# Decoder layer on one Trainium2 core: order of the prologue, copies into the stacks, and a narrower first score product

## The chip, the cores and the metric

The kernel runs on one NeuronCore of a Trainium2 chip. The core has TensorE (PE, matrix products into PSUM), VectorE (DVE), ScalarE (ACT), GpSimd (POOL) and SyncE (SP); in this kernel SP only issues transfers, nearly all of them, in one queue that is worked in program order. The metric is the device time of one launch in microseconds (us). Lower is better.

## The reference

One decoder layer over 64 sequences of 256 tokens with 256 features, with a context of 120 tokens per sequence, all in float32:

```python
x = x + self_attention(layernorm(x))          # 16 heads of 16, bias -slope_h * |i - j|, causal
x = x + cross_attention(layernorm(x), ctx)    # 16 heads of 16 over the 120 context tokens, no mask
x = x + tanh(layernorm(x) @ W @ A1 @ A2 + bias)
```

Self-attention of one head is `softmax(q @ k.T / 4 + bias) @ v`, where a key later than the query is excluded (minus infinity). So for 256 queries and 256 keys the quarter "first 128 queries, last 128 keys" is excluded as a whole, and two quarters are cut along their diagonal.

## The kernel before, in words

**The precision scheme.** Most products run in a rounded 32-bit format (`fp32r` in the trace's operand column of what is written, `f32` in that of a matmul). An operand is split into a high half, rounded by ScalarE (`hi`, line 774), and a low half, the rest, made by VectorE (`lo`, line 920). A semaphore `K_hi`, `Q_hi`, `XQ_hi` counts the high halves and `K_lo`, `Q_lo`, `XQ_lo` the low ones. VectorE works on a block only after ScalarE has.

**The stacks.** For scores the 16 dimensions of a head are laid out 128 partitions high in `q_stack` and `k_stack` (two of each, for even and odd sequences) and in `xq_stack` and `xk_stack`. In each group of 8 rows, rows 0, 4 and 1 (`TRIPLE`) hold high and low halves of the 16 dimensions; rows 2, 3, 5 and 6 (`STEPS`) hold constants whose products make the causal mask; 7 and 15 hold the distance bias; the last row holds the shift, minus the row's maximum. So one matmul gives the shifted, biased and masked score. `restack` (line 422) fills the three rows of `TRIPLE` by three transfers of 256 KB each, from `q_nat` or `k_nat`: before it issues any, SP waits for the low half, and for the last reader of the stack.

**The mask constants.** `steps_q` and `steps_k` (lines 1062 to 1073, GpSimd) hold 64 patterns over 256 tokens, four tokens to a pattern (`NSTEP = 4`). `set_rows(p)` (line 367) copies them, the ones and the bias rows into the stacks of parity p with 11 transfers, of which 8 are of 256 KB.

**Score products.** For each head `scores` (line 617) does two matmuls into one PSUM bank: keys 128 to 255 against all 256 queries (line 622), and keys 0 to 127 against all 256 queries (line 623). The exponential (line 805) reads columns 128 to 511 of the bank, so not the first 128 columns, the excluded quarter. `maxima` (line 576) forms the same scores in bf16 for the row maxima, on stacks without the shift row; VectorE reduces them (line 962), `MAX_T` transposes them (line 613), ScalarE copies them out (line 844) and SP's `MAX_STACK` (line 435) puts them into the shift row with two transfers.

**Order of the work.** Nothing is planned at run time: `ORDER` (line 65) is for each engine a list of steps with an offset in sequences, and every engine walks its list for t from -2 to 65, so that three sequences are under way at a time. All engines take their instructions strictly in program order. For t from 6 to 61 the walk is a hardware loop of two sequences.

**The prologue.** It differs from the loop in what is put around it. SP first loads x, all weights, the bias rows (`alibi`, in four pieces) and the biases in the order of line 354. PE, ACT and DVE turn and split the weights of `FIRST` (q, k and two of the feed-forward weights); then each engine walks its list; and in front of the first step that `comes_first` (line 296) does not let through, it runs `after_first`: on PE, ACT and DVE `other_weights`, the rest of the weights; on SP `other_rows` (line 388), that is a wait for three tiles zeroed by GpSimd, `set_rows(1)` and one more transfer; on POOL `other_zeroes` (line 1081), the zeroing of `k_stack[1]`, `q_stack[1]` and `xk_stack`. Before its walk ACT waits for the bias rows, all nine biases and the scaled biases (lines 763 to 765); DVE waits for the nine biases and scales two of them (lines 910 to 913); POOL waits for the nine biases (line 1078).

SP's list for a step t is `LOAD_X` (t+1), `MAX_STACK` (t), `XK_STACK` (t-1), `LOAD_CTX` (t), `XQ_STACK` (t-1), `K_STACK` (t+1), `Q_STACK` (t+1), `XMAX_STACK` (t-1), `STORE` (t-2), `XK_SAVE` (t). POOL's is `FFN` (t-2), `LN2` (t), `LN1` (t+2), `LN3` (t-1). Of a sequence's 16 `SCORE` steps in PE's list, six stand right behind a product whose operands are all in the rounded format: heads 1, 3, 7, 8, 9 and 11.

Of the kernel before, what the change touches and what calls it, by code (L numbers as in the profile page):

```python
# [31 lines left out]
ALU = mybir.AluOpType  # L32
# [7 lines left out]
H = 16  # L40
# [9 lines left out]
NSTEP = 4  # L50
UP = [2.0 ** (57 - 38 * p) for p in range(NSTEP)]
DOWN = [0.0] + [-2.0 ** (38 * p - 82) for p in range(1, NSTEP)]
BEYOND = -2.0 ** 70
# [115 lines left out]
def build(nc, x, ctx, wts, bias, alibi, out):  # L169
    turns = bank_turns()  # L170
    with ExitStack() as stack:
# [37 lines left out]
        steps_q = sb("steps_q", [T // NSTEP, T])  # L209
        steps_k = sb("steps_k", [T // NSTEP, T])  # L210
# [85 lines left out]
        def comes_first(kind, b):  # L296

            return kind in ("LOAD_X", "LOAD_CTX", "LN1", "LN1_T", "K", "Q") or \
                kind in ("K_STACK", "Q_STACK") and b == 0

        def walk(eng, name, do, after_first):

            def step(i, t):
                for kind, b, part in step_order(name, t):
                    do[kind](i, b, part)
            waiting = True
            for t in range(FIRST_STEP, LOOP_FROM):
                for kind, b, part in step_order(name, t):
                    if waiting and not comes_first(kind, b):
# [42 lines left out]
        def _(sp):  # L352
            sp.dma_start(x_in[0][:, :, :], x[0].rearrange("(a p) d -> p a d", p=P)).then_inc(sem("x_loaded0"), 16)
            for n in ["q", "k", "alibi", "f1", "f0", "f2", "v", "o", "xq", "xk", "xv", "xo"]:
# [12 lines left out]
            def set_rows(p):  # L367
# [7 lines left out]
                for stacks, made in ((q_stack, steps_q), (k_stack, steps_k)):  # L375
                    for n, row in enumerate(STEPS):
                        sp.dma_start(stacks[p][row:P:ROWSTEP, :, :].bitcast(F32),
                                     made[n::NSTEP, :].unsqueeze(1).to_broadcast([P // ROWSTEP, H, T]))\
                            .then_inc(set_, 16)
# [5 lines left out]
            sp.wait_ge(sem("steps_cut"), 2)  # L385
# [58 lines left out]
            def store(i, b, _):  # L444
# [7 lines left out]
                "Q_STACK": restack("q", "Q_lo", q_nat, q_stack, (0, 0, 1)),  # L452
                "K_STACK": restack("k", "K_lo", k_nat, k_stack, (0, 1, 0)),
                "XQ_STACK": restack("xq", "XQ_lo", q_nat, [xq_stack] * 2, (0, 0, 1)),
# [9 lines left out]
        def _(pe):  # L464
# [26 lines left out]
            def other_weights():  # L491

                first = [(k, b) for t in range(FIRST_STEP, LOOP_FROM) for k, b, _ in step_order("PE", t)]
                first = first[:[comes_first(k, b) for k, b in first].index(False)]
# [122 lines left out]
            def scores(i, b, h):  # L617
# [4 lines left out]
                pe.matmul(bk[:, 0:T], ks[:, h, P:T], qs[:, h, :], start=True, stop=True)  # L622
# [109 lines left out]
        def _(act):  # L732
# [41 lines left out]
            def hi(kind, free):  # L774
# [3 lines left out]
                def f(i, b, _):  # L778
# [4 lines left out]
                    free(i, b)  # L783
                    bk = blocks(bank_of(kind, i, b))
# [93 lines left out]
        def _(dve):  # L878
# [33 lines left out]
            dve.tensor_scalar(bcol["xq"][:, :], bcol["xq"][:, :], SCALE["xq"], None, ALU.mult)\  # L912
                .then_inc(sem("b_scaled"), 1)
# [6 lines left out]
            def lo(kind):  # L920
# [3 lines left out]
                def f(i, b, _):  # L924
                    if kind in ("CTX_T", "XK"):
# [130 lines left out]
        def _(pool):  # L1056
# [5 lines left out]
            for p in range(NSTEP):  # L1062
                pool.memset(steps_q[:, p::NSTEP], UP[p]).then_inc(sem("steps_laid"), 1)
                pool.memset(steps_k[:, p::NSTEP], DOWN[p]).then_inc(sem("steps_laid"), 1)
            pool.wait_ge(sem("steps_laid"), 2 * NSTEP)
            for tile in (steps_q, steps_k):
                pool.affine_select(out=tile[:, :], in_=tile[:, :], compare_op=ALU.is_ge, fill=0.0, base=0,
                                   pattern=[[1, T]], channel_multiplier=-NSTEP).then_inc(sem("steps_from"), 1)
            pool.wait_ge(sem("steps_from"), 2)
            for tile, beyond in ((steps_q, 0.0), (steps_k, BEYOND)):  # L1070
                pool.affine_select(out=tile[:, :], in_=tile[:, :], compare_op=ALU.is_ge, fill=beyond,
                                   base=NSTEP - 1, pattern=[[-1, T]], channel_multiplier=NSTEP)\
                    .then_inc(sem("steps_cut"), 1)
# [4 lines left out]
            pool.wait_ge(sem("b_loaded"), 16 * 9)  # L1078
# [8 lines left out]
            def normalise(kind, src, dst, free, bias_name, biased):  # L1087
# [3 lines left out]
                def f(i, b, _):  # L1091
# [84 lines left out]
```

## Time and profile before

| | |
|---|---|
| median of three runs | 2411.53 us (2410.28 to 2416.39) |
| the profiled execution | 2413.22 us |
| its span, first to last instruction | 2411.4 us |
| PE busy | 2235.1 us, 93% |
| PE weight loads busy | 1850.9 us, 77% |
| DVE, ACT, POOL busy | 1710.2, 1416.4, 719.4 us |
| DMA | 244.83 MB moved, mean 102 GB/s |
| mean granted TensorE clock | 0.979 of 2.4 GHz |

The span is the time from the first to the last instruction; the profiled execution's own time is 1.8 us more. A group of instructions in the profile shows its line, engine, operation and operands. Matmuls overlap: the recorded duration of one is longer than the distance from its start to the next one's start. The chain of waits gives a matmul the time by which it moved the chain on, and so does not count the overlap.

### The profile page before, as it was taken

Reading aid. Unit: us, or ns where it says so; the run is one execution under the profiler, and the core shown is the slowest. Engines: PE = TensorE matmul, PEld = TensorE weight load, DVE = VectorE, ACT = ScalarE, POOL = GpSimd, SP = SyncE. Lnnn points to the kernel's source line nnn. Section 1 sums busy time; section 2 is a strip of 40 time slices with the busy share of each in tenths; the row PEclk is TensorE's granted clock in tenths of the full one; section 3 lists DMA queues with packets and bytes.
Section 4 is the critical chain, followed back from the end, with each engine's and each line's share of the span. In section 5 each row is a group of like instructions: output and inputs, shape, how many; then the busy total and the mean of one; then the engine's idle time right before and its main releaser. Section 6 shows DMA issues by size and latency. Waiting matters only on the chain.

```text
span 2411.4 us, 67050 instructions
## 1 busy us (share of the span) xinstructions
PE 2235.1 (93%) x22072; PEld 1850.9 (77%) x22072; DVE 1710.2 (71%) x3710; ACT 1416.4 (59%) x3066; POOL 719.4 (30%) x1371
## 2 busy tenths in 40 slices
PE   3489999999999999999999999999999999999985
PEld 2367887887788788788878878887887888788774
DVE  3167777777777777777777778777777877777762
ACT  2246666666666666666666666666666666666651
POOL 1223233233333323323332332333233233323321
PEclk9699999999999999999999999999999999999996
DMA  7333443443343344334334433433443343344320
GB/s 126 76 81 104 115 109 95 111 109 97 99 118 105 97 111 109 96 100 118 104 98 111 109 93 102 115 103 101 111 109 89 106 114 101 105 111 109 89 81 22
DMA packets 167370, 244.83 MB, mean 102 GB/s; under 512 B 22176, under 2 KB 90512, under 8 KB 164248
## 3 DMA queue, kind: packets, MB, share of 16 engines
q1 hardware_dynamic: 165660, 244.22, 38.2%
q8 instruction: 28, 0.46, 0.1%
q10 hardware_dynamic: 1664, 0.01, 0.1%
q14 instruction: 18, 0.15, 0.0%
HBM read 53.13 MB, written 33.56 MB: 36 GB/s over the span
## 4 chain that ended last, share of the span: by engine, by line
PE 74%; DVE 8%; POOL 4%; DMA 4%; issue 4%; SPq 2%; ACT 2%; DVEq 0%; POOLq 0%; ACTq 0%
PE ps_misc L534 13%; PE ps_misc L548 13%; PE ps_score L622 7%; PE ps_max L605 5%; PE ps_score L632 5%; PE ps_score L623 4%; PE ps_attend L647 4%; PE ps_misc L677 4%; DVE neg_max_s L962 4%; PE ps_max L593 4%; PE ps_misc L518 3%; PE ps_misc L692 3%; PE ps_attend L666 2%; DMA q_stack<-neg_max_t_s 2%; PE ps_misc L559 2%
## 5 line engine op out<-in xcount | busy, mean ns | idle before, releaser
L805 ACT ACTIVATE probs<-ps_score 128x384 f32<-128x384 f32 x1024 | 476.0, 494 | 177.4 <-PE ps_score L623 174.2
L962 DVE TENSOR_REDUCE neg_max_s<-ps_max 128x2 f32<-128x512 f32 (+1 forms) x768 | 479.5, 680 | 5.5 <-PE ps_max L587 4.1
L812 ACT ACTIVATE xprobs<-ps_score 120x512 f32<-120x512 f32 x512 | 292.4, 597 | 251.9 <-PE ps_score L632 213.8
L622 PE MATMUL ps_score<-q_stack,k_stack 128*128 128x256 f32 x1024 | 343.0, 345 | 46.4 <-DMA q_stack<-neg_max_t_s 42.3
L1095 POOL TENSOR_SCALAR ve_LN<-mv_LN 128x2 f32<-128x2 f32 x192 | 37.0, 193 | 1152.1 <-DVE mv_LN L984 1146.5
L970 DVE TENSOR_REDUCE neg_max_x<-ps_max 128x4 f32<-128x480 f32 x512 | 317.0, 651 | 25.7 <-PE ps_max L605 14.1
L623 PE MATMUL ps_score<-q_stack,k_stack 128*128 128x256 f32 x1024 | 279.6, 281 | 0.0
L622 PEld LDWEIGHTS ps_score<-q_stack,k_stack 128*128 128x128 f32 x1024 | 194.1, 190 | 92.3 <-DMA q_stack<-neg_max_t_s 58.5
L632 PE MATMUL ps_score<-xq_stack,xk_stack 128*120 128x256 f32 x1024 | 201.7, 309 | 3.7 <-DMA xq_stack<-neg_max_t_x 2.8
L1121 POOL TENSOR_TENSOR res<-res,chain_n 128x512 f32<-128x512 f32 x64 | 81.7, 1276 | 412.6 <-ACT chain_n L850 412.6
L593 PE MATMUL ps_max<-k_stack,q_stack 127*128 127x256 bf16 x1024 | 195.7, 282 | 4.1 <-DVE neg_max_s L962 0.6
L623 PEld LDWEIGHTS ps_score<-q_stack,k_stack 128*128 128x128 f32 x1024 | 196.3, 192 | 0.0
L605 PE MATMUL ps_max<-xk_stack,xq_stack 127*128 127x120 bf16 x2048 | 183.7, 219 | 5.8 <-DMA xq_stack<-q_nat 5.3
L632 PEld LDWEIGHTS ps_score<-xq_stack,xk_stack 128*120 128x120 f32 x1024 | 138.9, 183 | 59.7 <-ACT xprobs L812 27.7
L936 DVE TENSOR_TENSOR chain_t<-ps_misc,chain_t 128x512 fp32r<-128x512 f32 x128 | 88.2, 689 | 119.0 <-ACT chain_t L790 119.0
L822 ACT ACTIVATE heads_t<-ps_attend 128x512 f32<-128x512 f32 x256 | 152.7, 597 | 24.3 <-PE ps_attend L666 15.5
L677 PE MATMUL ps_misc<-ident,heads_t 128*128 128x128 f32 x1024 | 159.8, 279 | 6.3 <-ACT heads_t L822 1.8
L647 PE MATMUL ps_attend<-probs,v_aug 128*32 128x256 f32 x2048 | 164.4, 393 | 0.0
L945 DVE SCALAR_TENSOR_TENSOR q_nat<-ps_misc,bias_xq,q_nat 128x256 fp32r<-128x256 f32 x128 | 56.1, 479 | 145.0 <-ACT q_nat L798 145.0
L666 PE MATMUL ps_attend<-xprobs,xv_aug 120*32 120x256 f32 x2048 | 152.1, 392 | 2.4 <-ACT heads_t L822 1.4
L1109 POOL TENSOR_SCALAR chain_n<-res,rstd_LN,nmr_LN 128x256 f32<-128x256 f32 x256 | 141.2, 559 | 27.1 <-POOL nmr_LN L1104 27.1
L605 PEld LDWEIGHTS ps_max<-xk_stack,xq_stack 127*128 127x128 bf16 x2048 | 120.4, 98 | 27.5 <-DVE neg_max_x L970 6.3
(147 smaller groups left out, 5394.0 us busy)
## 6 DMA issues: line engine op xcount, KB each, us to landing
k_stack<-k_nat SPq DMA_DIRECT2D x192, 256.0 KB, 3.6
q_stack<-q_nat SPq DMA_DIRECT2D x192, 256.0 KB, 3.7
xq_stack<-q_nat SPq DMA_DIRECT2D x192, 256.0 KB, 3.7
xk_stack<-scr_xk SPq DMA_DIRECT2D x192, 128.0 KB, 2.7
x_in<-in_x SPq DMA_DIRECT2D x64, 256.0 KB, 2.7
scr_xk<-k_nat SPq DMA_DIRECT2D x32, 512.0 KB, 3.0
out_y<-res SPq DMA_DIRECT2D x64, 256.0 KB, 2.2
ctx_in<-in_ctx SPq DMA_DIRECT2D x32, 240.0 KB, 3.0
```

The lines of the kernel that those rows point to most:

```text
L534: mm = pe.matmul(bk[:, m, :], wt[w][:, k, m * P:(m + 1) * P], src_t(h, k), start=(k == 0 and n == 0), stop=(k == NB - 1 and n == 2))
L548: mm = pe.matmul(bk[:, m, :], src_t(h, k)[:, m * P:(m + 1) * P], wt[w][:, k, :], start=(k == 0 and n == 0), stop=(k == NB - 1 and n == 2))
L593: mm = pe.matmul(two[:, j, :], narrow(qs[0:SHIFT, h, P:T]), narrow(ks[0:SHIFT, h, :]), start=True, stop=True)
L605: mm = pe.matmul(bk[:, j * C:(j + 1) * C], narrow(xq_stack[0:SHIFT, h, qb * P:(qb + 1) * P]), narrow(xk_stack[0:SHIFT, b % 2, h, 0:C]), st ...
L622: pe.matmul(bk[:, 0:T], ks[:, h, P:T], qs[:, h, :], start=True, stop=True)
L623: pe.matmul(bk[:, T:2 * T], ks[:, h, 0:P], qs[:, h, :], start=True, stop=True)\
L632: mm = pe.matmul(bk[0:C, j * T:(j + 1) * T], xk_stack[:, b % 2, h, 0:C], xq_stack[:, h, :], start=True, stop=True)
L647: pe.matmul(bk[32 * j:32 * j + 32, at:at + T], v_aug[b % 2][:, 0, h * VW:h * VW + 32], probs[:, h % 8, P:3 * P], start=True, stop=False, s ...
L805: act.activation(probs[:, h % 8, :], bank_of("SCORE", i, b, h)[:, P:4 * P], ACT.Exp)\
L812: act.activation(xprobs[0:C, at:at + 2, :], blocks(bank_of("XSCORE", i, b, u))[0:C], ACT.Exp).then_inc(sem("xprobs_ready"), 1)
L962: dve.tensor_reduce(o, ins, AX.X, ALU.max, negate=True).then_inc(sem("max_taken"), 1)
L970: dve.tensor_reduce(neg_max["x"][:, qb, 4 * g:4 * g + 4], bk, AX.X, ALU.max, negate=True).then_inc(sem("xmax_taken"), 1)
```

## The change

It has four parts.

1. **Mask and first score matmul.** `NSTEP` is 2, and the 64 patterns now cover 128 tokens each, separately for the two halves of a sequence, with constants of their own for each half. The constants no longer give a usable value in the excluded quarter, and line 622 now computes keys 128 to 255 against queries 128 to 255 only. There are as many patterns, rows and transfers as before. GpSimd has one more instruction to make them.
2. **The stacks' copies.** `restack` waits for the high half, issues its two copies, then waits for the low half and issues the third.
3. **What comes first.** `comes_first` depends on the engine. SP now lets through everything up to the first `XK_STACK` or the first `K_STACK` or `Q_STACK` of sequence 1, so that `MAX_STACK` of sequence 0 and `LOAD_CTX` stand ahead of `other_rows`. POOL lets through sequence 0 alone, so that `other_zeroes` stands ahead of the layernorm of sequence 1. On PE, ACT and DVE the rest of the weights stays where it was.
4. **Gates and loads.** The bias rows are loaded ahead of the weights. ACT's three waits move in front of its first K; DVE's wait and scaling of biases move in front of the low half of the first `LN1_T`; POOL's wait moves in front of the first addition of a bias.

```diff
-NSTEP = 4
-UP = [2.0 ** (57 - 38 * p) for p in range(NSTEP)]
-DOWN = [0.0] + [-2.0 ** (38 * p - 82) for p in range(1, NSTEP)]
-BEYOND = -2.0 ** 70
+NSTEP = 2
+UP = [[2.0 ** (70 - 90 * a - 45 * p) for p in range(NSTEP)] for a in range(2)]
+DOWN = [[0.0, -2.0 ** (90 * a - 55)] for a in range(2)]
+BEYOND = [-2.0 ** (90 * a - 10) for a in range(2)]
...
-        def comes_first(kind, b):
-            return kind in ("LOAD_X", "LOAD_CTX", "LN1", "LN1_T", "K", "Q") or \
-                kind in ("K_STACK", "Q_STACK") and b == 0
+        def comes_first(name, kind, b):
+            if name == "SP":
+                return kind not in ("K_STACK", "Q_STACK", "XK_STACK") or b == 0 and kind != "XK_STACK"
+            if name == "POOL":
+                return b == 0
+            return kind in ("LN1", "LN1_T", "K", "Q")
...
-            for n in ["q", "k", "alibi", "f1", "f0", "f2", "v", "o", "xq", "xk", "xv", "xo"]:
+            for n in ["alibi", "q", "k", "f1", "f0", "f2", "v", "o", "xq", "xk", "xv", "xo"]:
...
             def restack(name, made, nat, stacks, halves):
                 def f(i, b, _):
-                    wait(sp, made, 1, i, b, 1)
+                    wait(sp, f"{made}_hi", 1, i, b, 1)
                     if name == "xq":
+                        if isinstance(i, int) and b == 0:
+                            sp.wait_ge(sem("rows_set1"), 16 * 12)
                         wait(sp, "xscores_ready", 8, i, b)
                     else:
                         wait(sp, "scores_ready", 16, i, b - 1)
-                    for row, half_ in zip(TRIPLE, halves):
+                    for row, half_ in sorted(zip(TRIPLE, halves), key=lambda x: x[1]):
+                        if half_ == 1:
+                            wait(sp, f"{made}_lo", 1, i, b, 1)
                         sp.dma_start(stacks[b % 2][row:P:ROWSTEP, :, :]...
...
-                pe.matmul(bk[:, 0:T], ks[:, h, P:T], qs[:, h, :], start=True, stop=True)
+                pe.matmul(bk[:, P:T], ks[:, h, P:T], qs[:, h, P:T], start=True, stop=True)
...
-            act.wait_ge(sem("alibi_copied"), 1)
-            act.wait_ge(sem("b_loaded"), 16 * 9)
-            act.wait_ge(sem("b_scaled"), 1)
...
+                    if isinstance(i, int) and kind in ("K", "Q") and b == 0:
+                        act.wait_ge(sem("alibi_copied"), 1)
+                        act.wait_ge(sem("b_loaded"), 16 * 9)
+                        act.wait_ge(sem("b_scaled"), 1)
...
-            dve.wait_ge(sem("b_loaded"), 16 * 9)
-            dve.tensor_scalar(bcol["q"][:, :], bcol["q"][:, :], SCALE["q"], None, ALU.mult)
+            def scale_biases():
+                dve.wait_ge(sem("b_loaded"), 16 * 9)
+                dve.tensor_scalar(bcol["q"][:, :], bcol["q"][:, :], SCALE["q"], None, ALU.mult)
...
+                    if isinstance(i, int) and kind == "LN1_T" and b == 0:
+                        scale_biases()
...
-            pool.wait_ge(sem("b_loaded"), 16 * 9)
             pool.wait_ge(sem("half_made"), 1)
...
+                        if isinstance(i, int) and b == 0:
+                            pool.wait_ge(sem("b_loaded"), 16 * 9)
```

## Rows read from the trace of the kernel before

**Rows 1.** Stretches: length; busy us (count) of PE, PEld, DVE, ACT, POOL; clock, DMA, GB/s.
```profile
56.00:100.00 44.00, 11.19 (x55) 7.21 (x56) 8.29 (x16) 2.26 (x6) 14.01 (x10) 0.57 0.24 56
1000.00:1500.00 500.00, 485.92 (x4891) 404.30 (x4890) 376.89 (x820) 311.29 (x674) 155.12 (x295) 1.00 0.39 104
```

**Rows 2.** What PE waited for from 300 to 2270 us: total, times, longest.
```profile
PE ps_misc L518 <- POOL chain_n L1109: 37.2, 56, 0.7
PE ps_score L622 <- DMA q_stack<-neg_max_t_s: 9.9, 53, 0.2
```

**Rows 3.** Chain of waits, prologue: start us, us, what.
```profile
20.61 7.92 DMA bias_xv<-in_b_xv
28.79 0.67 DVE st_LN L980 x2
...
55.91 0.42 PE ps_max L587 x4
...
76.53 3.46 POOL xk_stack L1085
...
97.20 0.58 PE ps_score L622
...
129.36 0.30 PE ps_misc L613
...
132.47 0.39 PE ps_score L622
```

**Rows 4.** Timeline of the prologue: start us, us, engine, line, operation, operands, count.
```profile
18.74 2.77 DVE L885 CAST xq_stack<-k_nat 2x1024 fp32r<-2x1024 f32 x4 [9.24 <-DMA k_nat<-in_alibi]
22.48 1.97 PE L473 MATMUL ps_misc<-ident,res 128*128 128x128 f32 x8 [7.23 <-DVE w_q_lo L896]
28.68 5.87 SPq L377 DMA_DIRECT2D k_stack<-steps_k  x4
35.09 0.69 DVE L936 TENSOR_TENSOR self_t<-ps_misc,self_t 128x512 fp32r<-128x512 f32 x1 [5.26 <-ACT self_t L790]
40.59 1.84 SPq L430 DMA_DIRECT2D k_stack<-k_nat  x3
64.85 0.41 PE L613 MATMUL ps_misc<-ident,neg_max_s 128*32 128x128 f32 x1
93.62 2.27 SPq L439 DMA_DIRECT2D q_stack<-neg_max_t_s  x2
106.54 1.87 SPq L430 DMA_DIRECT2D k_stack<-k_nat  x3
116.25 0.54 PE L587 MATMUL ps_max<-k_stack,q_stack 127*128 127x128 bf16 x4 [2.19 <-DMA q_stack<-q_nat]
```

**Rows 5.** Transfers from 0 to 60 us, GB/s in 40 slices of 1.5 us.
```profile
GB/s 0 165 226 57 32 49 52 171 44 45 75 112 348 352 336 226 75 178 217 201 203 181 203 205 89 1 0 31 294 231 198 242 225 3 0 0 0 11 0 0
```

**Rows 6.** What PE waited for: first line 0 to 300 us, second from 2270 us on.
```profile
PE ps_max L587 <- DMA q_stack<-q_nat: 3.7, 2, 2.2
PE ps_max L605 <- DMA xq_stack<-q_nat: 5.1, 3, 2.7
```

**Rows 7.** Chain of waits in the loop, what each group moved it on.
```profile
1200.02 0.12 PE ps_score L622
...
1203.45 0.23 PE ps_max L605 x4
1203.68 0.17 PE ps_score L622
...
1205.01 0.22 PE ps_attend L651 x8
...
1207.33 0.44 PE ps_misc L518 x4
```

**Rows 8.** Timeline of weight loads in the loop.
```profile
1203.47 0.19 PEld L622 LDWEIGHTS ps_score<-q_stack,k_stack 128*128 128x128 f32 x1
1203.58 0.19 PEld L623 LDWEIGHTS ps_score<-q_stack,k_stack 128*128 128x128 f32 x1
```

More of the change, by code:

```diff
@@ L208, in build @@
         ones_row = sb("ones_row", [2, T])
-        steps_q = sb("steps_q", [T // NSTEP, T])
-        steps_k = sb("steps_k", [T // NSTEP, T])
+        steps_q = sb("steps_q", [P // NSTEP, T])
+        steps_k = sb("steps_k", [P // NSTEP, T])
         neg_max = {n: sb(f"neg_max_{n}", [P, NB, H]) for n in ("s", "x")}
@@ L308, in walk @@
                 for kind, b, part in step_order(name, t):
-                    if waiting and not comes_first(kind, b):
+                    if waiting and not comes_first(name, kind, b):
                         after_first()
@@ L377, in set_rows @@
                         sp.dma_start(stacks[p][row:P:ROWSTEP, :, :].bitcast(F32),
-                                     made[n::NSTEP, :].unsqueeze(1).to_broadcast([P // ROWSTEP, H, T]))\
+                                     made[n::len(STEPS), :].unsqueeze(1).to_broadcast([P // ROWSTEP, H, T]))\
                             .then_inc(set_, 16)
@@ L384, in _ @@
             sp.wait_ge(sem("ones_made"), 1)
-            sp.wait_ge(sem("steps_cut"), 2)
+            sp.wait_ge(sem("steps_cut"), 3)
             set_rows(0)
@@ L451, in _ @@
                 "XK_SAVE": save_xk, "XK_STACK": restack_xk,
-                "Q_STACK": restack("q", "Q_lo", q_nat, q_stack, (0, 0, 1)),
-                "K_STACK": restack("k", "K_lo", k_nat, k_stack, (0, 1, 0)),
-                "XQ_STACK": restack("xq", "XQ_lo", q_nat, [xq_stack] * 2, (0, 0, 1)),
+                "Q_STACK": restack("q", "Q", q_nat, q_stack, (0, 0, 1)),
+                "K_STACK": restack("k", "K", k_nat, k_stack, (0, 1, 0)),
+                "XQ_STACK": restack("xq", "XQ", q_nat, [xq_stack] * 2, (0, 0, 1)),
                 "MAX_STACK": stack_max("s", lambda b: q_stack[b % 2]),
@@ L493, in other_weights @@
                 first = [(k, b) for t in range(FIRST_STEP, LOOP_FROM) for k, b, _ in step_order("PE", t)]
-                first = first[:[comes_first(k, b) for k, b in first].index(False)]
+                first = first[:[comes_first("PE", k, b) for k, b in first].index(False)]
                 pe.wait_ge(sem("w_loaded_f2"), 16)
@@ L909, in _ @@
                 weight_rest(n, nm, banks["misc"][n % 2])
[L910 to L913 removed]
+            def scale_biases():
+                dve.wait_ge(sem("b_loaded"), 16 * 9)
+                dve.tensor_scalar(bcol["q"][:, :], bcol["q"][:, :], SCALE["q"], None, ALU.mult)
+                dve.tensor_scalar(bcol["xq"][:, :], bcol["xq"][:, :], SCALE["xq"], None, ALU.mult)\
+                    .then_inc(sem("b_scaled"), 1)
             def other_weights():
@@ L1061, in _ @@
             pool.memset(ones_row[:, :], 1.0).then_inc(sem("ones_made"), 1)
[L1062 to L1065, printed above, removed]
+            for a in range(NB):
+                for p in range(NSTEP):
+                    at = slice(a * P + p, (a + 1) * P, NSTEP)
+                    pool.memset(steps_q[:, at], UP[a][p]).then_inc(sem("steps_laid"), 1)
+                    pool.memset(steps_k[:, at], DOWN[a][p]).then_inc(sem("steps_laid"), 1)
+            pool.wait_ge(sem("steps_laid"), 4 * NSTEP)
             for tile in (steps_q, steps_k):
-                pool.affine_select(out=tile[:, :], in_=tile[:, :], compare_op=ALU.is_ge, fill=0.0, base=0,
-                                   pattern=[[1, T]], channel_multiplier=-NSTEP).then_inc(sem("steps_from"), 1)
+                pool.affine_select(out=blocks(tile), in_=blocks(tile), compare_op=ALU.is_ge, fill=0.0, base=0,
+                                   pattern=[[0, NB], [1, P]], channel_multiplier=-NSTEP)\
+                    .then_inc(sem("steps_from"), 1)
             pool.wait_ge(sem("steps_from"), 2)
[L1070 to L1073, printed above, removed]
+            pool.affine_select(out=blocks(steps_q), in_=blocks(steps_q), compare_op=ALU.is_ge, fill=0.0,
+                               base=NSTEP - 1, pattern=[[0, NB], [-1, P]], channel_multiplier=NSTEP)\
+                .then_inc(sem("steps_cut"), 1)
+            for a in range(NB):
+                part = steps_k[:, a * P:(a + 1) * P]
+                pool.affine_select(out=part, in_=part, compare_op=ALU.is_ge, fill=BEYOND[a], base=NSTEP - 1,
+                                   pattern=[[-1, P]], channel_multiplier=NSTEP).then_inc(sem("steps_cut"), 1)
             pool.memset(ctx_t[:, :, :, :, :].bitcast(F32), 0.0).then_inc(sem("ctx_zeroed"), 1)
```

## The prediction

> **What bounds the kernel now.** First the stretches of the span: from 1000 to 1500 us PE is busy 485.92 of 500 us at the full clock, while DVE, ACT and POOL have much room [rows 1]. Next what PE waits for in the loop: from 300 to 2270 us only 37.2 us for POOL's normalised rows before a transpose and 9.9 us for the shift row [rows 2]. Neither is a wait for the three-row copies into a stack. So the loop goes at the pace of PE's own instructions, and a copy that lands earlier there finds nobody waiting.
>
> Then the ends. From 56 to 100 us PE is busy 11.19 of 44 us [rows 1]. The chain of waits says why [rows 3]: MAX of sequence 0 starts at 55.91, and POOL zeroes the odd stacks only after the layernorm of sequence 1, the third memset running from 76.53 to 80.00; only then does SP issue the rows of the odd stacks, with the shift rows of sequence 0 queued behind them at 93.62 [rows 4], and the first score product runs at 97.20. Yet the transpose of the maxima that the shift needs was at 64.85 [rows 4]. Earlier the chain runs over the last bias transfer, issued at 20.61 and landed 7.92 later, which holds up DVE's first layernorm (28.79) [rows 3].
>
> The change can act in three places: the prologue, PE's cost of the first score product (1024 times), and the few waits for stacks at the two ends. I add up against the profiled execution, 2413.22 us, which is 1.69 above the median of the three runs.
>
> **a. The shift of sequence 0 no longer waits for the odd stacks.** In sequence 1 the way from this transpose to the first score takes 132.47 - 129.36 = 3.11 us (copy, two issues, landing) [rows 3]. For sequence 0, 64.85 + 3.11 = 67.96 instead of 97.20: -29.2 us. What is late next is below, in c. The memsets (3 of some 3.5 us) move to between the two layernorms on POOL, ending at about 40; the layernorm of sequence 1 waits for DVE, which takes it up after its first maxima, and MAX of sequence 0 started at 55.91 [rows 3], so even 7 us earlier the memsets are covered and cost nothing. If they were not covered, all of their 10.4 us would stand ahead of that layernorm, which is itself needed only after the fourth score.
>
> **b. The gates.** Without the bias gate DVE's first layernorm waits for the weights of `FIRST`. These are late themselves: their last products start at 22.48 and take 1.97, because DVE reaches the weights only after the bias rows (cast from 18.74, for 2.77) [rows 4]. With the bias rows first in the queue the cast runs earlier, but q's and k's weights land later by as much as the four small transfers took. I put the last copy of `FIRST` at about 23.2 (k's rest at 21.4 when its weights land at 18 or 19, a transpose of 1.0, a copy of 0.6), so the layernorm starts 5.5 us earlier, at 23.3. Bounds: 25.1 if the two feed-forward products stay where they are (gain 3.7), or 21.5 (gain 7.3). The gate still holds DVE's scaling, at 28.5, but it now stands in front of the low half of LN1_T, which comes at 35.09 - 5.5 = 29.6 [rows 4]; ACT's K comes after it, and POOL's bias addition feeds nothing near. If biases landed 2 us later, 1 to 2 us of the gain would go. I take -5.5, range -2 to -7. All that follows up to the first score, 62.5, moves with it; SP has issued the last even row at 34.55 [rows 4], while K's low half was there at 40.59 [rows 4], its high half some 0.9 before, so now at 34.2: that just fits.
>
> **c. What comes late instead.** SP now issues the odd rows after the shift rows and the context. The shift's issues end at about 61.2, the context's (0.6) at 61.8, and the twelve transfers before took from the end of the memsets, 80.0, to 93.6 [rows 3, 4]: 61.8 + 13.6 = 75.4. Only then can K and Q of sequence 1 be stacked. Before, K's was issued 9.3 us after the first score (106.54 against 97.20) and MAX of sequence 1 started 19.05 after it (116.25) [rows 3, 4]; with the first score at 62.5 that would be 71.8 and 81.5. So K's is issued 3.6 us late, and its data stand behind the rows' data. When the even rows were sent, data still flowed some 3 us after the last issue, and such transfers moved at about 220 GB/s [rows 5]; six copies of 256 KB are 1.57 MB, 7.1 us. 75.4 + 2.9 + 7.1 = 85.4 against 81.5: +3.9 us. At least 0 (if the data overlap), at most +8 (the six copies at 150 GB/s, 10.5 us, with some 0.7 for the last to report).
>
> **d. Copies of the high half.** Half of the wait before a stack is used goes: the third transfer used to be issued 1.2 us after the low half (three issues in 1.87 [rows 4]), now at once. Where PE waits for it, that is worth about 1.2 us each. PE waited so twice before MAX, 3.7 us in all, of which the 2.2 of sequence 1 are dealt with in c, and three times before XMAX at the end, 5.1 us in all [rows 6]. -1.2 and -3.6: -4.8 us, at most 1.5 + 5.1 = 6.6, at least 2. In the loop: nothing, since no such wait is in [rows 2]. The extra wait on SP holds up only what SP would have held up too, as it waited for the low half before.
>
> **e. The narrower product.** No row shows a product in the rounded format with 128 moving columns. What is near: with 256 columns in a stream 0.12 us; the transposes, 128 columns and 128 x 128 weights of four bytes, 0.44 for 4, so 0.11; bf16, 128 columns and fewer, 0.23 for 4, so 0.057 [rows 7]. The weights tell which to choose: the next four-byte weights are loaded 0.11 us after the last (1203.47, 1203.58) [rows 8], also when no stream is in the way. Line 623's product needs its own weights, which load while line 622's streams. So the narrower product can free only 0.12 - 0.11 = 0.01 us, and only in a stream; after another kind of product the pair already waits for its weights (0.17 for line 622 [rows 7]). Six of 16 heads stand in a stream: 64 x 6 x 0.011 = -4.2 us. Bounds: -11 (all 1024), and on the other side a format that slows at this width, a rival below.
>
> The Trainium skill (TensorE: Matmul & The Clock Gate, Back-to-back issue gap) gives a gap of N / 2.4 + 2.5 ns, thus 56 ns for 128 columns. As an estimate by that page the product would save over 50 us in all. Against it stand the weight loads at 0.11 [rows 8] and the transposes at that same 0.11.
>
> **Sum.** -29.2 - 5.5 + 3.9 - 4.8 - 4.2 = -39.8: 2373.4 for a profiled execution, 2371.7 for the median; I say 2372.
>
> **The rivals.**
> - *R1, the narrow product is slow (slower than before).* Place: line 622, 1024 times. If the rounded format at 128 columns runs as plain four-byte products do, its price is 0.22 (line 651: 128 columns, four products side by side, so one product's time [rows 7]). In place of 0.12 that is +0.10 each, +102 us; with the rest of the sum (-35.6) 2411.5 + 66.8 = 2478. For it: the trace has this format only with 256 columns. Against it: at 256 columns it costs 0.12 and no row hints at a width in which its pace changes. The turning point is 0.15 us: above that it eats the prologue's 35.6. 12%.
> - *R2, the narrow product saves its columns in full.* 0.057 instead of 0.12, 1024 times: -65 us in place of -4.2, so 2311. It needs weight loads that are quicker than 0.11, against [rows 8]. This is what the page's gap would come to. 4%.
> - *R3, the prologue gives back much of it.* Rows of the odd stacks, K and Q of sequence 1, the first exponentials and the context come together, PE falls to half its clock (0.57 of full between 56 and 100 [rows 1]), or the gates bring nothing, since q's and k's weights come later. c at +12 instead of +3.9 and b at -2 instead of -5.5: 2371.7 + 11.6 = 2383; up to 2397 if the second sequence loses as much. 14%.
> - *R4, the changes don't reach the end of the prologue.* MAX of sequence 1 could be held by something that I don't see until near its old time. Then within 0.3% of before. Against it: all its inputs hang on the first score or on SP's queue. 3%.
>
> **How the numbers follow.** Forecast 67%, R1 12, R2 4, R3 14, R4 3. The forecast's own range is 2357 to 2386: terms at their best -29.2 - 7 + 0 - 6.6 - 11 = -53.8, at their worst -29.2 - 2 + 8 - 2 = -25.2. R3 carries it up to 2397. Range 2357 to 2397, leaving out R1, R2, R4. A measurement of this kernel tells 0.3% (7 us) from no change. Faster by more: forecast, R2, R3 and a part of R1 in which the price is below the turning point: 0.85. Within: 0.04. Slower: 0.11.
>
> **What would show it.** a: the first score product at 60 to 65 us, and no SP issue of odd rows ahead of its shift rows. b: DVE's first layernorm at 22 to 25. c: MAX of sequence 1 at 82 to 89, PE waiting for a stack before it, with SP's K copies right behind the rows. d: the waits before XMAX at the end near 1.5 us in all; in the copies, two issues, then one after the low half. e: line 622 at 128x128 with the start of line 623 some 0.11 behind it in a stream, and 35.2 us for a sequence in the loop, as before, or up to 0.1 less. I am wrong at the root if a sequence in the loop takes over 0.3 us more or less than before.

## The result, and the profile after

| | before | after |
|---|---|---|
| median, runs | 2412.73 us (2410.28 to 2416.39, 4 runs) | 2376.95 us (2373.22 to 2378.05, 4 runs) |
| profiled execution, its span | 2413.22, 2411.4 us | 2373.22, 2371.5 us |
| mean granted TensorE clock | 0.979 | 0.984 |

The ratio is 0.9841 [0.9829, 0.9853], which would be 38 us of 2412.73. The two medians differ by 35.8 us; in the larger group of runs further down (*after_again*, five beside nine) they differ by 38.9. So the gain is known to some 3 us. The profiled execution of after is also the quickest of its four, so where a size matters I also use the trace of a second run of the same kernel (*after_again* below; profiled at 2377.68 us, span 2375.9).

Stretches of after, as in [rows 1] (length; busy us and count of PE, PEld, DVE, ACT, POOL; clock, DMA share, GB/s):
```profile
56.00:100.00 44.00, 30.40 (x233) 24.06 (x234) 16.77 (x36) 15.80 (x36) 9.59 (x20) 0.82 0.48 120
1000.00:1500.00 500.00, 485.62 (x4888) 405.29 (x4886) 377.19 (x820) 311.10 (x674) 154.29 (x295) 1.00 0.40 105
```
The hole in the prologue has been filled: PE is busy for 30.40 of these 44 us, where it was busy for 11.19. The loop is as it was.

The timeline of after's prologue answers to [rows 4] (start us, us, engine, line, operation, operands, count, idle time before and its releaser):
```profile
10.03 2.77 DVE L893 CAST xq_stack<-k_nat 2x1024 fp32r<-2x1024 f32 x4 [0.53 <-DMA k_nat<-in_alibi]
14.13 2.23 PE L480 MATMUL ps_misc<-ident,probs 128*128 128x128 f32 x8 [14.13 <-DMA probs<-in_w_q]
17.01 2.26 PE L480 MATMUL ps_misc<-ident,res 128*128 128x128 f32 x8 [0.65 <-DVE w_q_lo L904]
19.95 0.75 DVE L993 BATCH_NORM_STATS2 st_LN<-x_in 128x6 f32<-128x256 f32 x2 [1.85 <-ACT xprobs L761]
25.89 0.17 DVE L922 TENSOR_SCALAR bias_q<-bias_q 128x2 f32<-128x2 f32 x1 [4.80 <-DMA bias_xv<-in_b_xv]
34.12 3.52 POOL L1103 MEMSET xk_stack<- 128x4096 f32 x1
54.07 0.28 PE L620 MATMUL ps_misc<-ident,neg_max_s 128*32 128x128 f32 x1
54.77 1.21 SPq L446 DMA_DIRECT2D q_stack<-neg_max_t_s  x2
56.66 0.72 SPq L374 DMA_DIRECT2D q_stack<-ones_row  x1
57.52 0.48 PE L629 MATMUL ps_score<-q_stack,k_stack 128*128 128x128 f32 x1 [3.16 <-DMA q_stack<-neg_max_t_s]
68.80 1.35 SPq L395 DMA_DIRECT2D xk_stack<-ones_row  x1
70.19 3.03 SPq L437 DMA_DIRECT2D k_stack<-k_nat  x3
```
The first layernorm on DVE starts at 19.95, the memsets end at 37.64, the transpose of the maxima is at 54.07 and its first score at 57.52: 3.45 us apart, where they were 32.35 apart [rows 4, 3]. The rows of the odd stacks (issued from 56.66 on) now stand between that score and K of sequence 1 (70.19).

What PE waited for in after; the columns are total, times and longest. The first line is from 0 to 300 us, the next two from 265 to 2230, the last from 2230 on, and they answer to [rows 6] and [rows 2]:
```profile
PE ps_max L594 <- DMA q_stack<-q_nat: 6.7, 2, 5.8
...
PE ps_misc L525 <- POOL chain_n L1127: 37.2, 56, 0.7
PE ps_score L629 <- DMA q_stack<-neg_max_t_s: 8.5, 44, 0.2
...
PE ps_max L612 <- DMA xq_stack<-q_nat: 1.7, 2, 0.9
```
The wait for the stack of sequence 1 has become longer (5.8 against 2.2), that for the cross stacks at the end shorter (1.7 against 5.1), and in the loop nothing has changed.

The chain of waits in after's loop (start, what it moved the chain on), for [rows 7]:
```profile
1200.02 0.12 PE ps_score L629
1200.13 0.17 PE ps_score L630
1200.31 0.06 PE ps_score L629
1200.37 0.17 PE ps_score L630
```
In a stream the narrow product moves the chain on by 0.06 and the wide one behind it by 0.17: 0.23 for the pair. Two sequences of the loop take 70.36 us, before 70.465.

### The profile page after: what moved, and what is told of

Read it like the earlier page. It is cut to its first block, busy times and chain, and to the rows that moved or that the text cites. A ratio compares the mean times of both kernels' runs of the same rounds, so it can differ in the third digit from the quotient of the medians.

```text
span 2371.5 us, 67224 instructions
## 1 busy us (share of the span) xinstructions
PE 2229.0 (94%) x22072; PEld 1848.5 (78%) x22072; DVE 1708.8 (72%) x3710; ACT 1416.2 (60%) x3066; POOL 719.2 (30%) x1372
## 4 chain that ended last, share of the span: by engine, by line
PE 75%; DVE 8%; issue 5%; POOL 4%; DMA 3%; ACT 2%; SPq 2%; DVEq 0%; POOLq 0%; ACTq 0%
PE ps_misc L555 14%; PE ps_misc L541 14%; PE ps_score L630 7%; PE ps_max L612 5%; PE ps_score L639 5%; PE ps_score L629 4%; PE ps_attend L654 4%; PE ps_misc L684 4%; DVE neg_max_s L975 4%; PE ps_max L600 3%; PE ps_misc L525 3%; PE ps_misc L699 3%; PE ps_attend L673 2%; DMA q_stack<-neg_max_t_s 2%; PE ps_misc L566 2%
## 5 line engine op out<-in xcount | busy, mean ns | idle before, releaser
L630 PE MATMUL ps_score<-q_stack,k_stack 128*128 128x256 f32 x1024 | 321.6, 335 | 0.0
L629 PE MATMUL ps_score<-q_stack,k_stack 128*128 128x128 f32 x1024 | 292.6, 286 | 17.7 <-DMA q_stack<-neg_max_t_s 12.3
L830 ACT ACTIVATE heads_t<-ps_attend 128x512 f32<-128x512 f32 x256 | 152.7, 597 | 24.3 <-PE ps_attend L673 15.5
L1116 POOL TENSOR_TENSOR rstd_LN<-ve_LN,half 128x2 f32<-128x2 f32 x192 | 134.7, 702 | 16.0
```

The costliest lines, as they stand in the source:

```text
L629: pe.matmul(bk[:, P:T], ks[:, h, P:T], qs[:, h, P:T], start=True, stop=True)
L630: pe.matmul(bk[:, T:2 * T], ks[:, h, 0:P], qs[:, h, :], start=True, stop=True)\
```

## The experiments

All are edits of the changed kernel. They were run in three groups, each on a chip of its own and beside nine runs of the kernel before, which a ratio refers to. First group (median of before 2416.58 us): after_again, e_oldorder, e_rowsfirst, e_gates. Second (2416.66): e_alibi, e_lowait, e_wide, e_twice. Third (2417.44): e_twice64, rowsfirst_again, e_rows_lowait, e_best. "More" and "less" are differences of medians from after_again, and in the third group from rowsfirst_again; those of the second group are therefore taken across two chips.

**after_again**: no edit.

> The changed kernel once more, on the chip and beside the runs of the kernel before that the next three are compared with. Expected 2374 to 2379 us and a ratio of 0.983 to 0.985 to before.

Measured: 2377.68 us (5 runs) against 2416.58, ratio 0.9838 [0.9825, 0.9852]. This is the reference for the first two groups. In its trace q's weights land later: PE's first wait for them lasts 16.9 us, in the profiled after 14.1. Its first layernorm is at 22.59 and its first score at 61.59.

**e_oldorder**: the odd stacks again ahead of the shift of sequence 0, on SP and on POOL.

```diff
-                return kind not in ("K_STACK", "Q_STACK", "XK_STACK") or b == 0 and kind != "XK_STACK"
+                return kind in ("LOAD_X", "LOAD_CTX") or kind in ("K_STACK", "Q_STACK") and b == 0
             if name == "POOL":
-                return b == 0
+                return kind == "LN1"
```

> The changed kernel with the old order of what comes first on SP and GpSimd: zeroing behind the layernorm of sequence 1, odd rows ahead of the shift rows of sequence 0; gates, loads, stacks' copies and the narrower product as changed. Theory (29 of the gain is this wait, 4 came back): zeroing would run from 60.0 to 70.4, the rows to 84.0, the first score at about 87.7 instead of 57.5 (+30.2), and the 4 us of lateness in sequence 1 go: +26 us, about 2402. Rival (the order brings less, and gates, copies and the product the rest): +15 or less, about 2391.

Measured: 2402.49, ratio 0.9941 [0.9928, 0.9955], 24.8 more than after_again. Its timeline, columns as above:
```profile
70.55 3.51 POOL L1103 MEMSET xk_stack<- 128x4096 f32 x1
74.08 0.71 SPq L374 DMA_DIRECT2D q_stack<-ones_row  x1
87.70 2.28 SPq L446 DMA_DIRECT2D q_stack<-neg_max_t_s  x2
91.29 0.48 PE L629 MATMUL ps_score<-q_stack,k_stack 128*128 128x128 f32 x1 [33.23 <-DMA q_stack<-neg_max_t_s]
```
The pattern of [rows 3, 4] is back: memsets, rows right behind them, the shift 13.6 us after the first of these, and PE waits for 33.2 us. The first score is 29.7 us later than in after_again. By MAX of sequence 1 (109.78 against 84.24) 25.5 of it are left, and that is what the median shows: part of the order's gain is given back by late rows.

**e_rowsfirst**: only SP's line of that edit, so POOL zeroes early and SP issues the odd rows before the shift.

```diff
-                return kind not in ("K_STACK", "Q_STACK", "XK_STACK") or b == 0 and kind != "XK_STACK"
+                return kind in ("LOAD_X", "LOAD_CTX") or kind in ("K_STACK", "Q_STACK") and b == 0
```

> The changed kernel with one edit: SP issues the odd stacks' rows right after sequence 0's stacks and the load of x (some 38 us), in the idle stretch before the shift rows of sequence 0 (54.8), and no longer behind them. GpSimd has zeroed the tiles by 37.6. Theory (the rows were what came late instead, 4 us): K and Q of sequence 1 are stacked at once when they are made, the wait for a stack before MAX of sequence 1 (5.8 us in the trace of the changed kernel) falls to about 2, first score of sequence 1 near 93 us instead of 96.8, time 3 to 4 us less than the changed kernel. Rival 1 (that wait has another cause, K and Q themselves or a clock at half speed): same time as the changed kernel within 1 us. Rival 2 (the rows now run into the shift rows of sequence 0): first score of sequence 0 later than 57.5 by 2 us or more, time the same or more.

Measured: 2371.82, ratio 0.9814 [0.9801, 0.9827], 5.9 less than after_again, where 3 to 4 less was expected. Its timeline:
```profile
40.76 0.71 SPq L374 DMA_DIRECT2D q_stack<-ones_row  x1
53.41 1.33 SPq L395 DMA_DIRECT2D xk_stack<-ones_row  x1
58.91 1.18 SPq L446 DMA_DIRECT2D q_stack<-neg_max_t_s  x2
70.38 1.94 SPq L437 DMA_DIRECT2D k_stack<-k_nat  x3
```
The rows go out from 40.76 to 54.74, in a stretch in which SP has nothing else, and the shift is not delayed (first score 61.73, after_again 61.59). MAX of sequence 1 comes at 79.91 instead of 84.24, and its first score at 95.20 instead of 101.23: 6.0 us, which is what the median shows. So of the two halves of part 3 only POOL's is needed; SP's own half costs what it was meant to avoid.

**e_gates**: the three gates where they were before; bias rows still first in the load order.

```diff
+            act.wait_ge(sem("alibi_copied"), 1)
+            act.wait_ge(sem("b_loaded"), 16 * 9)
+            act.wait_ge(sem("b_scaled"), 1)
...
+            dve.wait_ge(sem("b_loaded"), 16 * 9)
...
+            pool.wait_ge(sem("b_loaded"), 16 * 9)
```

> The changed kernel with the old gates: DVE and GpSimd wait for all nine biases before their first layernorm and ACT before its walk; the bias rows are still loaded first. Theory (the layernorm started 8.8 us earlier since both the bias gate and the late weights went): DVE's first layernorm at about 26.1, when the last bias has landed, instead of 19.95, so all later steps 6 us later, time 6 us more than the changed kernel, about 2382. Rival (the waits merely moved, since the scaling and K stand behind the same biases): 1 us or less.

Measured: 2382.99, ratio 0.9856 [0.9841, 0.9871], 5.3 more. Single runs of the two kernels overlap (2378.49 to 2386.14 against 2374.84 to 2381.69), so the trace has to carry it. DVE in its timeline:
```profile
29.41 0.17 DVE L920 TENSOR_SCALAR bias_q<-bias_q 128x2 f32<-128x2 f32 x1 [8.23 <-DMA bias_xk<-scr_bias]
29.56 0.75 DVE L989 BATCH_NORM_STATS2 st_LN<-x_in 128x6 f32<-128x256 f32 x2
```
The layernorm stands behind the biases again, 7.0 us later than in after_again, and the first score (68.56) too.

**e_alibi**: the load order as before, gates moved.

```diff
-            for n in ["alibi", "q", "k", "f1", "f0", "f2", "v", "o", "xq", "xk", "xv", "xo"]:
+            for n in ["q", "k", "alibi", "f1", "f0", "f2", "v", "o", "xq", "xk", "xv", "xo"]:
```

> The changed kernel with the bias rows loaded behind the weights of q and k, as before, and the new gates. Theory (the first layernorm on DVE waits for the later of the gate and the weights of FIRST, and these wait behind the cast of the bias rows): the last copy of FIRST at about 25 again and the first layernorm at 25.1 in place of 20 to 22.6, time 2.5 to 5 us more than the changed kernel. Rival (the order of the loads changes nothing, only the gates do): within 1 us.

Measured: 2379.03, ratio 0.9842 [0.9828, 0.9855], 1.4 more. Its timeline:
```profile
19.16 2.77 DVE L893 CAST xq_stack<-k_nat 2x1024 fp32r<-2x1024 f32 x4 [9.65 <-DMA k_nat<-in_alibi]
22.90 1.97 PE L480 MATMUL ps_misc<-ident,res 128*128 128x128 f32 x8 [6.05 <-DVE w_q_lo L904]
25.54 0.75 DVE L993 BATCH_NORM_STATS2 st_LN<-x_in 128x6 f32<-128x256 f32 x2 [1.91 <-ACT xprobs L761]
```
The cast, then the weights, then the layernorm at 25.54, close to the 25.1 that the prediction gave as the bound without this step. The first score is 2.6 us later in the trace; the medians are 1.4 apart and the ratios overlap, so the time alone does not show the gain of the load order.

**e_lowait**: SP waits for the low half before it issues any of the three copies.

```diff
-                    wait(sp, f"{made}_hi", 1, i, b, 1)
+                    wait(sp, f"{made}_lo", 1, i, b, 1)
...
-                    for row, half_ in sorted(zip(TRIPLE, halves), key=lambda x: x[1]):
-                        if half_ == 1:
-                            wait(sp, f"{made}_lo", 1, i, b, 1)
+                    for row, half_ in zip(TRIPLE, halves):
```

> The changed kernel, but SP waits for the low half before it issues any of the three copies, in the old order of the copies. Theory: the waits of PE for a stack ahead of XMAX at the end go from 1.7 back to some 5 us, the one ahead of MAX of sequence 2 from 0.9 to 1.5 or 2; the loop stays at 70.36 us for two sequences; time 4 to 5 us more than the changed kernel. Rival (the copies matter in the loop too, since stacks come free sooner): the loop slower by 0.1 us or more for two sequences, time 8 us more. Rival 2: the three copies' data bound the wait, not when the third is issued: 1 us or less.

Measured: 2386.43, ratio 0.9868 [0.9853, 0.9883], 8.7 more, where 4 to 5 were expected. PE's waits for stacks, 0 to 300 us and at the end:
```profile
PE ps_max L592 <- DMA q_stack<-q_nat: 8.2, 2, 6.4
...
PE ps_max L610 <- DMA xq_stack<-q_nat: 4.5, 3, 2.0
```
They are 1.8 and 2.6 us longer than in after_again (6.4 and 1.9), 4.4 in all, and the time grows by twice that. The stretch between the first scores of sequences 1 and 2 shows where some of the rest goes (columns as in [rows 1]), of after_again and then of e_lowait:
```profile
100.00:136.00 36.00, 32.28 (x305) 25.50 (x303) 21.04 (x46) 20.11 (x43) 8.21 (x15) 0.92 0.35 86
```
```profile
100.00:137.00 37.00, 32.67 (x296) 25.94 (x296) 20.44 (x41) 18.93 (x41) 6.75 (x14) 0.86 0.34 84
```
In e_lowait PE is busy a little longer with fewer instructions, at a clock of 0.86 instead of 0.92. Against after_again it is 0.5 us late at the first score of sequence 1, 3.2 at that of sequence 2, 6.9 at that of sequence 8, 7.3 at that of sequence 60, and 10.2 at the end. In the 3.7 us from sequence 2 to 8 PE is busy for 1.9 us more over the same 2064 products, at a clock of 0.99 instead of 1.00, and waits 1.3 us more for the shift row. But e_alibi, whose copies are those of the changed kernel, also loses 2.9 us there, so a part of this can be chance.

**e_wide**: the first score product over 256 queries again, into columns that nobody reads.

```diff
-                pe.matmul(bk[:, P:T], ks[:, h, P:T], qs[:, h, P:T], start=True, stop=True)
+                pe.matmul(bk[:, 0:T], ks[:, h, P:T], qs[:, h, :], start=True, stop=True)
```

> The changed kernel, but line 629 again over all 256 queries; the excluded quarter is computed, with the new constants, and nothing reads it. Theory (the next four-byte weights take 0.11 us to load and hide most of the saved columns): a pair of sequences in the loop 70.46 us as before in place of 70.36, time 3 to 4 us more than the changed kernel. Rival (saved columns count in full): 50 us or more. Second rival (the product costs nothing either way): within 1 us.

Measured: 2379.45, ratio 0.9838 [0.9824, 0.9851], 1.8 more, which the medians alone can't tell from nothing. The loop can: two sequences take 70.453 us, in the changed kernel 70.360 (before 70.465), so 3.0 us over 32 pairs. The ten traces with one narrow product for each head lie between 70.355 and 70.398, so the two with the wide one stand clear of them, by 1.8 to 3.5 us over the kernel. No run takes back the new mask constants alone, but e_wide, which keeps them, has the loop of before within 0.012 us.

**e_twice**: the narrow product issued twice.

```diff
+                pe.matmul(bk[:, P:T], ks[:, h, P:T], qs[:, h, P:T], start=True, stop=True)
```

> The changed kernel with line 629's narrow product issued twice in a row, with the same result; its weights are loaded again. It measures what one such product costs by itself. Theory (the four-byte weight load sets the pace): 1024 times 0.11 us, 113 us more than the changed kernel, about 2490. Rival (its 128 columns set the pace): 1024 times 0.055, 56 us, about 2434. Rival 2 (plain four-byte pace): 1024 times 0.22, 225 us, about 2603.

Measured: 2447.18 against 2416.66, ratio 1.0122 [1.0106, 1.0137], 69.5 more than after_again. That lies between the theory's 113 and the rival's 56, so the time settles nothing between them; the distances in a stream do. The stream in its timeline:
```profile
1234.32 0.22 PE L629 MATMUL ps_score<-q_stack,k_stack 128*128 128x128 f32 x1
1234.38 0.28 PE L630 MATMUL ps_score<-q_stack,k_stack 128*128 128x128 f32 x1
1234.50 0.33 PE L631 MATMUL ps_score<-q_stack,k_stack 128*128 128x256 f32 x1
1234.67 0.22 PE L629 MATMUL ps_score<-q_stack,k_stack 128*128 128x128 f32 x1
```
A head takes 0.35 us instead of 0.23: the added product costs 0.11 to 0.12 there. Its weight loads, in the same stretch:
```profile
1234.33 0.19 PEld L630 LDWEIGHTS ps_score<-q_stack,k_stack 128*128 128x128 f32 x1
```
The next two start at 1234.44 and 1234.55, 0.11 apart.

**e_twice64**: the added product over 64 queries only.

```diff
+                pe.matmul(bk[:, P + 64:T], ks[:, h, P:T], qs[:, h, P + 64:T], start=True, stop=True)
```

> The changed kernel with a second product behind line 629's that has the same weights but only the last 64 queries as moving columns; same result. Beside the run with the product of 128 columns twice (2447 us, and 0.11 us from start to start for the added one): theory (its weight load sets the pace, not its columns): the same, 0.11 from start to start, 2445 to 2449 us. Rival (columns): 64 columns less are 0.027 us each, 27 us less or, with the part of it that other waits take up, 17 less, about 2430.

Measured: 2449.95 against 2417.44, ratio 1.0135 [1.0118, 1.0153]. Its timeline:
```profile
1235.71 0.22 PE L629 MATMUL ps_score<-q_stack,k_stack 128*128 128x128 f32 x1
1235.77 0.25 PE L630 MATMUL ps_score<-q_stack,k_stack 128*128 128x64 f32 x1
1235.86 0.36 PE L631 MATMUL ps_score<-q_stack,k_stack 128*128 128x256 f32 x1
1236.06 0.22 PE L629 MATMUL ps_score<-q_stack,k_stack 128*128 128x128 f32 x1
```
Again 0.35 for a head, and 72.655 us for two sequences, against 72.648 in e_twice. Half the columns save nothing: the columns do not set the price, and the loads of the weights, 0.11 apart, account for it.

**rowsfirst_again**: e_rowsfirst once more, for the next two.

> The kernel with the odd rows issued ahead of the shift rows once more, beside the next two. Expected 2370 to 2373 us.

Measured: 2373.89 against 2417.44, ratio 0.9818 [0.9803, 0.9834].

**e_rows_lowait**: e_rowsfirst and e_lowait together.

> Odd rows issued ahead of the shift rows, and SP waits for the low half before it issues any of the three copies, as before. Without the rows in front of the stacks of sequence 1 this asks what the early copies of the high half are worth by themselves. Theory (8.7 us were measured for them beside late rows, 1.0 to 1.2 of it at each of the five or six places where PE waits for a stack, and the rest from TensorE at half clock in sequences 2 to 8 behind the longer waits): 5 to 9 us more than with early copies, 2377 to 2380, with more stretches at half clock between 100 and 260 us in its trace. Rival (the copies were worth that much only since the late rows had pushed them back): 2 us or less.

Measured: 2381.03, ratio 0.985 [0.9834, 0.9866], 7.1 more than rowsfirst_again. PE's waits for stacks, 0 to 300 us and at the end:
```profile
PE ps_max L592 <- DMA q_stack<-q_nat: 3.8, 2, 2.2
...
PE ps_max L610 <- DMA xq_stack<-q_nat: 5.2, 3, 2.8
```
In rowsfirst_again they are 0.9 and 2.6: 5.5 us of direct waits, so most of the difference. The 3.8 and 5.2 are nearly those of the kernel before, 3.7 and 5.1 [rows 6].

**e_best**: e_rowsfirst, with the four bias-row transfers issued by ACT, so that q's weights are second in SP's queue.

```diff
-                        sp.dma_start(k_nat[32 * part:32 * part + 2, :, :, :].rearrange("p h a t -> p (h a t)"),
...
+            for part in range(4):
+                act.dma_start(k_nat[32 * part:32 * part + 2, :, :, :].rearrange("p h a t -> p (h a t)"),
+                               alibi[:, part * 4 * T:(part + 1) * 4 * T]).then_inc(sem("alibi_loaded"), 16)
```

> Odd rows issued ahead of the shift rows, and the bias rows loaded from ScalarE's queue ahead of its small bias transfers, so that SP issues the weights of q and k 1.4 us sooner. Theory (PE's first 14 to 17 us are a wait for q's weights): first weights 1 to 2 us sooner, time 1 to 2 us less than with the early rows alone, 2369 to 2371. Rival (the transfer engines, not the issue, set when q's weights land, or the biases, now later, hold up LN1_T): same or up to 2 us more.

Measured: 2376.32, ratio 0.983 [0.9816, 0.9845], 2.4 more than rowsfirst_again, where 1 to 2 less was expected. Its timeline (ACTq is ACT issuing a transfer):
```profile
4.85 1.09 PE L477 MATMUL ps_misc<-ident,probs 128*128 128x128 f32 x4 [4.85 <-DMA probs<-in_w_q]
23.10 1.20 ACTq L769 DMA_DIRECT2D bias_xk<-scr_bias  x1
24.34 1.08 ACT L761 ACTIVATE xprobs<-ps_misc 128x512 f32<-128x512 f32 x2 [12.76 <-issue]
25.46 0.75 DVE L993 BATCH_NORM_STATS2 st_LN<-x_in 128x6 f32<-128x256 f32 x2 [11.45 <-ACT xprobs L761]
```
q's weights are there at 4.85, 12 us earlier, yet the layernorm starts 2.6 later than in rowsfirst_again: ACT's copy of a weight stands in ACT's queue behind its own issues of the biases, which end at 24.3. One wait took the other's place.

The best version is e_rowsfirst: the ratios are 0.9814 and 0.9818, against 0.9838 for the changed kernel on the same chip as the first.

## Why the prediction was right, and where it was not

The forecast was 2372, the median is 2376.95, inside the range and 5 above. By medians the change brings 35.8 of the 39.8 us of the sum, in the group of after_again 38.9. The traces of before and after_again, whose spans differ by 35.5 (those of before and after by 39.9), show where each came from:

| to this point | predicted so far | measured so far |
|---|---|---|
| transpose of the maxima, seq. 0 (b) | -5.5 | -6.7 |
| first score, seq. 0 (a) | -34.7 | -35.6 |
| first score, seq. 1 (c, part of d) | -32.0 | -31.2 |
| first score, seq. 60 (e) | about -36 | -35.9 |
| end (rest of d) | -39.8 | -35.5 |

**a** was right: 32.35 us between transpose and first score became 3.45 to 3.47, so -28.9 for -29.2. The memsets ended at 37.64 for "about 40" and held up nothing. e_oldorder takes this part back, and confirms what the sum said: order and lateness of the rows together are worth 25.3 by the prediction (29.2 less 3.9), 24.8 by the chip.

**b** was right in its mechanism, and its size hangs on a landing that varies. The layernorm, forecast at 22 to 25, came at 22.6 in after_again and 19.95 in the profiled run. At the transpose of the maxima that is a gain of 6.7 in the one and of 10.8 in the other, beyond the range of -2 to -7. e_gates shows the gates alone to be worth 5.3 (7.0 at the first score in the traces), and e_alibi that without the new load order the layernorm is at 25.5. The profiled after is quick mostly because its q weights came 2.8 us sooner, which isn't the change's doing: its layernorm is 2.6 us sooner, of 4.1 at the first score. So that in this one trace the total comes out as forecast (39.9 for 39.8) is luck: what b has too much there covers what d's part at the end does not bring.

**c** was right in its parts. The rows were issued in 13.5 us (13.6 said), K 12.67 after the first score (12.9 said, 9.3 before), and MAX of sequence 1 22.77 after it where it was 19.05: 3.7 later for 3.9. But the prediction took this for a price of the order, and it is not: e_rowsfirst pays none of it and keeps all of a. SP's queue was idle from 40.9 to 58.8 us in after_again, and by the prediction's own numbers (memsets over at about 40, transpose at about 59, rows in 13.6) the rows fitted there. The measurement was forecast, the better version next to it was not seen.

**d's part at the end is what the two traces do not show.** d was -4.8, of which -3.6 at the end. PE's waits before XMAX did fall as it said, from 5.1 to 1.9 or 1.7 us. But from the first score of sequence 60 to the end the kernel before takes 198.38 us and the changed one 198.78 (198.16 in the profiled run). The last 100 us of before and of after_again:
```profile
2311.00:2411.00 100.00, 66.78 (x510) 50.49 (x508) 37.34 (x84) 34.80 (x71) 18.26 (x35) 0.77 0.12 33
```
```profile
2276.00:2376.00 100.00, 67.56 (x492) 50.82 (x490) 35.07 (x80) 33.22 (x68) 18.20 (x35) 0.71 0.12 33
```
PE is busy longer for fewer instructions, at a granted clock of 0.71 instead of 0.77: more of this stretch was run at 1.2 GHz. Over the last 200 us the number of products is the same, and the two lines can be set side by side:
```profile
2211.40:2411.40 200.00, 163.09 (x1480) 131.41 (x1480) 110.97 (x243) 96.42 (x206) 49.15 (x93) 0.89 0.27 73
```
```profile
2175.90:2375.90 200.00, 165.34 (x1480) 133.47 (x1480) 110.59 (x242) 95.98 (x205) 48.61 (x92) 0.85 0.27 73
```
PE is busy for 2.25 us more, so most of the 3.2 us that the shorter waits gave went into slower products. What put the clock lower isn't settled. It isn't the narrow product (e_wide has the same 0.71 and takes 199.06 us), and it isn't the early copies either: e_lowait, which copies as before does, ends at 0.69 and takes 201.75. Also, before is known by one trace, and two runs of one kernel (e_rowsfirst, rowsfirst_again) take 196.99 and 198.75 for this stretch.

Taken away from the changed kernel, the same step is worth there about what the sum said: e_lowait and e_rows_lowait take 3.0 and 3.3 us more from the first score of sequence 60 to the end, for 3.6. Over the whole kernel it is worth more than 4.8, namely 8.7 or 7.1: 4.4 or 5.5 of that are waits for stacks, and in e_lowait a lower clock and longer waits for the shift row go with the rest. A second price of a wait, in the clock behind it, was not in the sum at all; how large it is, these runs don't fix.

**e** was right: -0.105 us for two sequences, 3.4 for all, for -4.2. One detail was wrong: the second product does not start 0.11 behind the first but 0.06, and what comes next stands 0.17 behind the second. The pair's 0.23 is as said, the length of two loads; why it splits so, no run here shows. The Trainium skill (TensorE: Matmul & The Clock Gate, Back-to-back issue gap) gives 56 ns for 128 columns as the gap of an isolated product, and says itself that this counts too little where each product brings its own weights. The 0.06 from the first to the second product agrees with it; the pair's 0.23 doesn't, and two loads at 0.11 account for it. So the prediction's estimate of over 50 us used that gap outside its own condition.

The rivals. R1 (0.22 for the narrow product) and R2 (its columns saved in full) are excluded: 0.06 and 0.17, and e_twice and e_twice64 with 0.11 to 0.12 for an added product of either width. R1's price was also misread: the 0.22 of line 651 [rows 7] is for eight products, two groups of four side by side, so 0.11 for a group; by that row the plain format gives no price above 0.12. R3 held in one point, the clock, but at the end of the kernel and not in the prologue, which ran at 0.82 where it had 0.57. R4 is excluded by MAX of sequence 1 at 80.29 or 84.24 instead of 116.25, and its first score at 96.78 or 101.23 instead of 132.47.

## What to carry to other kernels

When a block of transfers stands in the way, look first for the stretch in which its queue idles and move the block's inputs ahead (here the memsets on POOL); to push the block behind the urgent work only moves the lateness to the next consumer. A wait of PE at an end of the kernel costs its own length and can cost more through the clock: 8.7 us for 4.4 of waits in one comparison here, 7.1 for 5.5 in another. What its removal gives is as uncertain; don't book either without a row for the clock. Before narrowing a product, look at the distance of the weight loads behind it: with new weights for each product, columns below that distance cost nothing here.

## What the runs showed of the hardware

- An added product in the rounded format with weights of its own costs 0.11 to 0.12 us in a stream at 128 and at 64 columns (e_twice, e_twice64), the pace of its 128 x 128 four-byte weight loads (0.11).
- PE at 97% busy is not the only thing that sets the loop's pace. e_twice adds 1024 products of 0.11, which would be 113 us; the time grew by 69.5, and two sequences by 2.29 us, 0.072 for each product. The remaining 0.04 was taken up by waits that the profile doesn't show as idle, because the recorded durations of matmuls overlap. Two such places: from the start of a wide score product to the start of the head transposes behind it the loop has 0.40 us at the median in the changed kernel and 0.19 in e_twice, and to the transposes of `chain_n` 0.38 and 0.17. So cuts on PE too can bring less than their length.
- The landing of the first weights varies from one run of the same kernel to the next: PE waits for them for 14.1 us in after and 16.9 in after_again, and what follows in the prologue moves with it. Differences of 3 us in such a kernel need several runs on one chip.
